# Weighted sums of an attention kernel taken in halves of 256 columns behind every pair of score products

## What is computed

```python
x = x + 0.5 * ffn(layernorm(x), W, b)
h = layernorm(x)
Q, K, V = (h @ Wq + bq), (h @ Wk + bk), (h @ Wv + bv)      # 16 heads of 8
scores = einsum('bhqd,bhkd->bhqk', Q, K) / sqrt(8)
scores = scores + 0.3 * log(mask + 1e-6)                   # mask: sigmoid of sines, per head
out = einsum('bhqk,bhkd->bhqd', softmax(scores), V)
x = x + out.reshape(B, L, H) @ Wo + bo
x = x + 0.5 * ffn(layernorm(x), W, b)
```

## Time and profile before

| | |
|---|---|
| time, median of 3 runs (lowest to highest) | 971.29 us (967.44 to 976.59) |
| the profiled execution | 967.31 us, its span 965.4 us |
| mean granted clock of TensorE | 0.907 |
| PE busy | 752.2 us (78%) |
| PEld busy | 259.3 us (27%) |
| DVE busy | 519.1 us (54%) |
| ACT busy | 682.9 us (71%) |
| POOL busy | 178.5 us (18%) |

### The profile page before, as it was taken

One profiled execution on the slowest core, in us unless ns is written; L12 is line 12 of the kernel. 1 busy time (PEld: TensorE's weight loads), 2 busy tenths in 40 slices (PEclk: granted clock), 3 DMA queues, 4 the chain that ended last, 5 costly groups with the idle time before them and its releaser, 6 DMA issues.

```text
span 965.4 us, 12701 instructions
## 1 busy us (share of the span) xinstructions
PE 752.2 (78%) x4355; PEld 259.3 (27%) x4355; DVE 519.1 (54%) x1275; ACT 682.9 (71%) x823; POOL 178.5 (18%) x154
## 2 busy tenths in 40 slices
PE   0355942489998788999987989999789888998943
PEld 0031320023222221334322323333223222322323
DVE  8732433467454237656785376566754322565364
ACT  1387753388886687888875888887667888888810
POOL 0201642010333202003344020033350000020010
PEclk9985555599999899999998999999999999999986
DMA  6316586945576766554766766547577665464201
GB/s 167 65 77 271 202 323 231 326 146 157 171 248 222 247 213 194 180 178 155 237 220 216 245 211 185 167 166 225 179 258 245 203 194 167 148 199 127 100 8 47
DMA packets 78120, 181.54 MB, mean 188 GB/s; under 512 B 17712, under 2 KB 42320, under 8 KB 67920
## 3 DMA queue, kind: packets, MB, share of 16 engines
q1 hardware_dynamic: 78048, 180.64, 57.5%
HBM read 115.51 MB, written 65.11 MB: 187 GB/s over the span
## 4 chain that ended last, share of the span: by engine, by line
PE 45%; DVE 15%; ACT 11%; SPq 10%; DMA 10%; issue 8%; POOL 1%; DVEq 0%; POOLq 0%; ACTq 0%
PE S_PS L1393 17%; PE O_PS L1406 15%; DVE S_PS L1088 6%; ACT BIG L650 6%; DMA BIG<-shift_rows 5%; SPq L321 5%; PE F_PS L1303 3%; PE R_PS L1415 3%; PE S_PS L1570 2%; ACT BIG L695 2%; SPq L308 2%; PE P_PS L1303 1%; DMA BIG<-ln_masks 1%; DMA BIG<-in_L_attn_x 1%; PE F_PS L1298 1%
## 5 line engine op out<-in xcount | busy, mean ns | idle before, releaser
L650 ACT ACTIVATE BIG<-S_PS 128x1024 f32<-128x1024 f32 x512 | 508.4, 1023 | 168.0 <-PE S_PS L1393 166.3
L1393 PE MATMUL S_PS<-BIG 98*128 98x512 bf16 x1024 | 308.6, 395 | 95.6 <-DVE S_PS L1088 58.4
L1406 PE MATMUL O_PS<-BIG,VX 128*9 128x512 f32 x2048 | 273.3, 607 | 0.9 <-issue 0.9
L1088 DVE COPY S_PS<-BIG 128x1024 f32<-128x1024 f32 x128 | 152.1, 1224 | 151.8 <-ACT BIG L650 126.2
L1393 PEld LDWEIGHTS S_PS<-BIG 98*128 98x128 bf16 x1024 | 75.0, 99 | 362.7 <-ACT BIG L650 131.3
L518 POOL TENSOR_TENSOR XDT<-PART 128x512 bf16<-128x512 f32 x32 | 36.0, 1125 | 321.7 <-ACT PART L624 321.6
L1100 DVE RECIPROCAL RD<-R_PS 128x16 f32<-128x16 f32 x64 | 16.4, 257 | 127.3 <-PE R_PS L1415 126.8
L1406 PEld LDWEIGHTS O_PS<-BIG,VX 128*9 128x9 f32 x2048 | 30.9, 88 | 114.6 <-issue 99.3
L495 POOL TENSOR_TENSOR BIG<-BIG,BFH 128x512 f32<-128x512 f32 x16 | 21.9, 1399 | 210.2 <-DVE BIG L957 132.8
L495 POOL TENSOR_TENSOR X<-X,BFH 128x512 f32<-128x512 f32 x16 | 21.8, 1392 | 143.6 <-DVE BIG L957 73.1
L527 POOL TENSOR_TENSOR PART<-PART 128x512 f32<-128x512 f32 x32 | 37.0, 1157 | 60.0 <-DVE PART L1023 58.7
(11 more groups left out here) (162 smaller groups left out, 740.2 us busy)
## 6 DMA issues: line engine op xcount, KB each, us to landing
BIG<-ln_masks SPq DMA_DIRECT2D x62, 1024.0 KB, 6.6
BIG<-q_parts SPq DMA_DIRECT2D x64, 384.0 KB
BIG<-k_parts SPq DMA_DIRECT2D x64, 288.0 KB
ln_masks<-BIG SPq DMA_DIRECT2D x16, 1024.0 KB, 6.2
q_parts<-PART SPq DMA_DIRECT2D x12, 768.0 KB, 3.6
k_parts<-PART SPq DMA_DIRECT2D x24, 384.0 KB, 4.6
q_parts<-PART SPq DMA_DIRECT2D x12, 512.0 KB, 4.5
k_parts<-PART SPq DMA_DIRECT2D x24, 256.0 KB, 3.9
```

The source lines that it names most:

```text
L650: act.activation(E[:, h % 2, j, 2 * pair:2 * pair + 2, :], S_PS[:, pair, :, :], ACT.Exp, scale=LOG_WEIGHT)\
L1088: ve.tensor_copy(S_PS[:, pair, :, :], LNM[:, h % 2, 2 * pair:2 * pair + 2, :]).then_inc(s["seeded"], 1)
L1393: mm = pe.matmul(S_PS[:, pair, i, :], KT[0:ALL_ROWS, slot, K_COL[j], 128 * kb:128 * kb + 128], QT[0:ALL_ROWS, slot, j, :], start=False, st ...
L1406: mm = pe.matmul(O_PS[32 * j:32 * j + HD + 1, :], VX[:, slot_of(n), j, kb, h, :], E[:, h % 2, j, kb, :], start=kb == 0, stop=kb == T - 1)
```

## The change

`weighted` takes a further argument, `half`, and does 256 of the 512 columns. It is called behind the scores of every step (half 0 of block k // 2 behind the even steps, half 1 behind the odd ones) instead of behind every second. The waits stand ahead of half 0 alone, the signal `pv_done` behind half 1. Only half 0 of the first block has `start`, since that flag covers the whole bank; half 1's first product finds its columns cleared. In the general path and behind the last head both halves follow each other.

```diff
-            def weighted(n, m, h, kb):
-                if kb == 0:
+            def weighted(n, m, h, kb, half):
+                if kb == 0 and half == 0:
...
-                pe.wait_ge(s["e_ready"], STEPS * m + STEPS - 1 + kb // 2)
-                for j in range(QB):
-                    mm = pe.matmul(O_PS[32 * j:32 * j + HD + 1, :], VX[:, slot_of(n), j, kb, h, :],
-                                   E[:, h % 2, j, kb, :], start=kb == 0, stop=kb == T - 1)
-                mm.then_inc(s["pv_done"], 1)
+                if half == 0:
+                    pe.wait_ge(s["e_ready"], STEPS * m + STEPS - 1 + kb // 2)
+                cols = slice(L // 2 * half, L // 2 * half + L // 2)
+                for j in range(QB):
+                    mm = pe.matmul(O_PS[32 * j:32 * j + HD + 1, cols], VX[:, slot_of(n), j, kb, h, :],
+                                   E[:, h % 2, j, kb, cols], start=kb == 0 and half == 0, stop=kb == T - 1,
+                                   skip_group_check=True)
+                if half == 1:
+                    mm.then_inc(s["pv_done"], 1)
...
                     scores(m, k)
-                    if k % 2 and m >= 1:
-                        weighted((m - 1) // NH, m - 1, (m - 1) % NH, k // 2)
+                    if m >= 1:
+                        weighted((m - 1) // NH, m - 1, (m - 1) % NH, k // 2, k % 2)
...
             for kb in range(T):
-                weighted(NQ - 1, last, NH - 1, kb)
+                weighted(NQ - 1, last, NH - 1, kb, 0)
+                weighted(NQ - 1, last, NH - 1, kb, 1)
```

More of the change, by code:

```diff
@@ L1552, in general @@
                     for kb in range(T):
-                        weighted(n, m, h, kb)
+                        weighted(n, m, h, kb, 0)
+                        weighted(n, m, h, kb, 1)
                     pe.wait_ge(s["max_row"], u + 1)
```

## The result

The changed kernel is slower: 998.74 us median (993.44 to 1004.05, 4 runs) against 973.94 (967.44 to 978.11), a ratio of 1.0261 with a 95% interval of 1.0177 to 1.0345. Run again beside the experiments it was 1.0295 (1.022 to 1.037). Its profiled execution took 998.31 us around a span of 996.4, which is 31.0 us more than the span before. Forecast were 988 from the median, or 17 us more: the direction and the mechanism held, the sum was short by about a third against the medians and by nearly half against the profiled execution.

A forecast was written before the change was run, and what follows sets the result against it. Most of the time something waits for PE, 45% of the chain. Terms 1 + 7.7 + 3.3 + 4.9 + 0.6 = 17.5, less about 0.5, gave +17 us, from the median 971.29 to 988; range 973 to 1010.

The forecast's parts named there:

- part 1: Each wave as two halves: a half 0.64 us, 0.21 of it going in and out; 54 us more PE time.
- part 2: Clean head: half 0 fills the wait between S0 and S1, copy of O already over; +0.04 a head, +1 us.
- part 3: PE work at step 6, between S6 and the next S1, stands behind a half: +0.64, 12 times, 7.7 us.
- part 4: Heads 3 and 4 of three quarters, product ahead of the next S0: +0.55, six times, 3.3 us.
- part 5: Stalled heads, no gap for half 0: six at 0.5, and three after the last stalls at 0.63; 4.9 us.
- A: Rival: halves cost more than their columns and 0.21, something fixed per matmul; 1006 or 1012 us; chance 0.17.
- B: Rival: within 1%, the spill at steps 6 stays in slack; +7 us, 978; chance 0.20.
- C: Rival: faster, second halves do not pay the 0.21 for going in and out; -20 us, about 951; chance 0.13.

The follow-up runs named there:

- the split alone: Changed kernel with both halves behind the odd steps, where the whole wave stood: 971.92 us against 973.11 for the kernel before, ratio 0.9987.
- the early copy: Changed kernel, but ACT copies O out directly behind exponential 7, ahead of the background copy: 1000.51 us, a single time.
- the second trace: The changed kernel as it is, traced in its run beside the experiments: span 993.5 us, measured 996.89 us, 1.0295 of the kernel before.
- step 6 alone: Changed kernel without the half behind step 6's scores; both halves of the last block stand behind step 7's: 986.20 us, 1.0151 of the kernel before.

## Why the prediction was right, and what was sized wrong

**The price of a half (part 1): right.** 0.53 and 0.55 were forecast and measured, 52 of 54 us of PE time came, and the split alone cost 0.01 us a wave. The Trainium skill ("TensorEngine Tiling (Array Packing)", Key Properties) says that a change of the tiling mode drains TensorE; the fixed 0.13 out and 0.09 in agree with it. The 60 cycles that the same page of the Trainium skill gives each matmul (Instruction Overhead) are no addition here: the four last waves have 32 records more and take 3.57 (951.59 - 948.02) instead of 3.56:

```profile
948.02 3.64 PE L1410 MATMUL O_PS<-BIG,VX 128*9 128x256 f32 x64 [1.19 <-issue]
951.59 0.66 PE L1421 MATMUL R_PS<-IDENT,OTS 128*128 128x128 f32 x4
```

**The clean head (part 2): right in kind, +0.11 for +0.04.** 0.03 by the gap, 0.05 by the turn behind a half, the rest by ticks of 1.085. ACT's idle went from S2 to S5 as said. One sentence of it failed elsewhere: that half 0's wait for the copy of O is over was read off a clean head and taken to hold everywhere. In heads 4, 5, 20, 21, 36 and 37 ACT has a background copy ahead of it, which the wave behind S1 had never felt.

**Steps 6 (part 3): right, 0.64 forecast, 0.74 measured** (5.05 - 4.31), 0.1 of it the product behind column tiles, which the forecast had at 0.89 as behind scores and which takes 1.00 there; in heads 54 to 58 3.6 us where the working gives 4 x 0.64 + 5 x 0.04 = 2.8.

**Products ahead of S0 (part 4): the term that failed most, 7.4 for 3.3.** The three heads together take 34.99 instead of 32.54, 2.45 more, forecast 1.1. The copy of O is 0.79 of that (0.23 + 0.56 came back with the early copy). Products and turns directly behind halves are another part, which that variant did not bring back: with the half behind the background work the three heads take 34.59, 0.40 less. If the two don't overlap, 0.16 of the 1.35 beyond the forecast is left open.

**Stalls (part 5): 4.9 in the sum, and here the account is least sure.** The V product of head 11 is 7.79 behind S0 (315.87 - 308.08 by the chain), 0.62 more, against a forecast of 0.5 a piece. But the stretches with stalls (heads 6 to 15, 22 to 31 and 38 to 47) grew by 17.0 us in the first trace and by 12.6 in the second, where the working has at most 10.0 for them (4.9 and eight steps 6 at 0.64). Head 9 alone is 2.8 of it, 14.09 instead of 11.32; it restarted at the low clock, where before it had not. The window over that restart before (length, busy of each engine, PEclk, DMA share, GB/s):

```profile
274.50:278.50 4.00, 3.94 (x25) 0.88 (x25) 3.61 (x11) 3.30 (x5) 1.86 (x2) 1.00 0.77 251
```

and after, with the timeline's row of the S0 it restarts with:

```profile
278.00:282.00 4.00, 3.97 (x21) 0.61 (x22) 2.68 (x7) 1.98 (x3) 1.16 (x1) 0.50 0.66 231
```

```profile
278.03 1.03 PE L1393 MATMUL S_PS<-BIG 98*128 98x512 bf16 x2 [2.00 <-DMA BIG<-shift_rows]
```

PE had been idle for 2.00 us ahead of it, before for 1.21. In the second trace of the changed kernel head 9 started at full clock behind 2.48 us of idle, but the clock fell just behind that (0.80 from 280.3 to 282.3 us, 0.50 from 282.3 to 284.3), and the head took 12.67. Heads 6 to 15 grew there by 5.3 us instead of 8.8, so part of the 31 us of the first trace is chance. The clock isn't the bulk of the loss, though: from the mean granted clocks (0.907 before, 0.907 and 0.911 after) and the spans I estimate 180 us at the low level before, 185 in the first trace after and 177 in the second, 2 x (1 - clock) x span, and the second is still 28.1 us longer than before. How much the clock adds over many executions wasn't measured, and whether the later S7 makes the loads of a stalled head later was not taken apart.

**The rivals.** A fell with the split alone (0.9987). B (the spill at steps 6 stays in slack) fell: step 6 alone gave 10.7 us back. C (second halves go in and out for nothing) fell: 0.53 in and 0.55 to the next S behind a first and a second half alike.

**The sum.** Right in sign and mechanism, 17 where 25 (medians) to 31 (profiled executions) were measured, and parts 2 to 5 each came out larger than their terms, so no two errors cancelled. Of the 14 us between 17 and 31, the products ahead of S0 are 4 and the stretches with stalls 7 or more; in the second trace it is 4 and 3 or more of 11. The terms were made with background work priced as it stood behind scores, and with a wait that only the clean head had shown to be over.

## What to carry to other kernels

Cutting a piece of work finer to even out an engine pays only where the new piece falls into time in which the engine waits. Price the going over between tile shapes from a row, count it once for each piece on the path, and split only the piece that has a gap beside it: here one split of four made the kernel 1.0 to 1.7% faster, and all four made it 2.6 to 3.0% slower. A wait moved ahead has to be looked up in the heads with the most other work, not in the clean one.

## What the hardware did that was not expected

Leaving out half of the columns of the weighted sums gave 990.97 us in its single run, hardly less than the 993 to 1004 of the full work. The mean granted clock was 0.842 instead of 0.907. In clean stretches heads of 9.0 us at 1.00 stand beside heads of 11.9 at 0.71, though PE's records cover 7.61 us of the former and it does the same work in both: within a slow head the granted clock is 0.50 from 800 to 806 us and 1.00 again from 807, so it fell to its low level (1.2 GHz) and rose back to 2.4. In the kernel before and in the changed one the same stretch (752 to 812 us, 775 to 836) is at 1.00 throughout. So a shorter PE path can lose its gain to the clock; why the clock fell, no run here takes apart.

A float32 product or turn behind matmuls in four column tiles starts its matmuls as soon as scores would, but takes 0.10 and 0.05 us longer than behind scores. The traces show the weight load beside it, before and after (timelines of PEld, for the product at step 6):

```profile
830.24 1.08 PEld L1303 LDWEIGHTS F_PS<-WO,XDT 128*128 128x128 f32 x8
```

```profile
856.53 0.97 PEld L1303 LDWEIGHTS F_PS<-WO,XDT 128*128 128x128 f32 x8 [0.43 <-issue]
```

Behind scores the first weights of the product are loaded from 830.24 on, 0.21 us ahead of its first matmul (830.45) and while the scores still stream. Behind the half the load starts with the first matmul (856.53), so the first load isn't hidden. That the load is the whole of the 0.10 was not shown by a run of its own.
